# Layer 0's routing and experts in one block, weighing twenty passes behind the gate and up products

## The reference, cut to what matters

```python
scores = sigmoid(x @ gate_w.T)                       # 64 experts
grp = (scores + gate_bias).reshape(T, 8, 8)          # the best 4 of 8 groups by their two best
masked = where(group chosen, scores + gate_bias, 0)
rw = weights of the best 8 of 64, divided by their sum, x 2.5, else 0
routed = sum over e of rw[:, e] * ((silu(x @ Wg[e].T) * (x @ Wu[e].T)) @ Wd[e].T)
shared = (silu(x @ Sg.T) * (x @ Su.T)) @ Sd.T
x = layernorm(x + routed + shared)
```

## Time and profile before

| | |
|---|---|
| median of three executions | 1408.93 us |
| the profiled execution | 1402.02 us |
| its span, first to last instruction | 1400.3 us |
| busy: TensorE, VectorE, ScalarE, GpSimd | 1279.3, 1114.2, 898.5, 481.3 us |
| granted TensorE clock, mean | 0.946 |
| blocks of layer 0's routing and experts | from about 240.4 to about 692.3 us of the span |

### The profile page before, as it was taken

The page is one execution under the profiler, slowest core; times in us unless marked ns, Lnnn a source line. Parts: engine busy times, 40 slices in busy tenths (PEclk is TensorE's granted clock), DMA queues, the critical chain, the costliest instruction groups (busy, mean ns, idle before and its releaser), DMA issues. The chain is left out here.

```text
span 1400.3 us, 21389 instructions
## 1 busy us (share of the span) xinstructions
PE 1279.3 (91%) x7374; PEld 711.9 (51%) x7374; DVE 1114.2 (80%) x1726; ACT 898.5 (64%) x1503; POOL 481.3 (34%) x988
## 2 busy tenths in 40 slices
PE   5898987169999999999889999999999998999998
PEld 2222224157777777777643232223222337777776
DVE  5677763758999999999758788888889747688886
ACT  4988873034555555555453788888888866767775
POOL 4565551014334343334142244224422422221210
PEclk8898988579999999999999999999999999999999
DMA  5422200064666666666236555434342201121200
GB/s 156 127 56 66 63 21 7 0 134 110 147 143 154 148 151 151 147 146 152 79 113 146 111 156 133 121 102 104 88 123 61 53 11 52 62 91 46 91 31 31
DMA packets 70020, 135.87 MB, mean 97 GB/s; under 512 B 13031, under 2 KB 44328, under 8 KB 63112
## 3 DMA queue, kind: packets, MB, share of 16 engines
q1 hardware_dynamic: 68760, 133.46, 37.5%
q10 hardware_dynamic: 1152, 1.05, 0.2%
HBM read 116.87 MB, written 16.29 MB: 95 GB/s over the span
## 5 line engine op out<-in xcount | busy, mean ns | idle before, releaser
L1589 ACT ACTIVATE a_PR<-n1a_C 128x512 f32<-128x512 f32 x576 | 299.6, 603 | 79.5 <-PE n1a_C L1495 79.4
L1604 DVE CUSTOM_DVE_ANT_0 OC_last<-a_mring,a_COR 128x1024 bf16<-128x1024 f32 x256 | 302.6, 1218 | 42.4 <-PE a_mring L1462 42.1
L1432 POOL TENSOR_SCALAR_AFFINE_SELECT a_PR<-a_PR 128x128 f32<-128x128 f32 x512 | 136.2, 296 | 250.2 <-ACT a_PR L1589 249.7
L868 ACT ACTIVATE e_HH<-e_H 128x512 fp32r<-128x512 f32 x184 | 116.4, 633 | 158.3 <-DVE e_H L916 157.5
L1495 PE MATMUL n1a_C<-a_QP,a_KP 74*128 74x512 bf16 (+3 forms) x768 | 176.1, 332 | 4.4 <-ACT a_PR L1589 3.5
L402 ACT ACTIVATE a_PR<-a_ring,a_ng 128x1024 f32<-128x1024 f32 (+1 forms) x160 | 150.2, 1045 | 26.0 <-PE a_ring L345 26.0
L427 DVE TENSOR_SCALAR a_PR<-a_PR,a_lo,a_hi 128x1024 f32<-128x1024 f32 (+1 forms) x160 | 119.2, 763 | 56.1 <-ACT a_PR L402 55.6
L1514 PE MATMUL n1a_C<-a_PR,a_V 128*9 128x512 f32 (+3 forms) x1536 | 152.1, 492 | 0.0
L887 DVE TENSOR_TENSOR e_HL<-e_H,e_HH 128x512 fp32r<-128x512 f32 x138 | 139.4, 1010 | 13.5 <-DVE e_H L904 0.5
L810 POOL TENSOR_TENSOR e_HL<-e_H,e_HH 128x512 fp32r<-128x512 f32 x46 | 78.5, 1706 | 180.5 <-ACT e_HH L868 180.5
L1883 DVE TENSOR_TENSOR e_HL<-e_GL,e_HH 128x512 fp32r<-128x512 f32 x144 | 109.5, 765 | 38.3 <-ACT e_HH L1851 34.7
(11 more groups left out here) (257 smaller groups left out, 2252.6 us busy)
## 6 DMA issues: line engine op xcount, KB each, us to landing
e_ROUTE<-routing SPq DMA_DIRECT2D x24, 704.0 KB
a_QP<-q_parts SPq DMA_DIRECT2D x72, 192.0 KB
e_RAW<-in_w_chunks SPq DMA_DIRECT2D x46, 192.0 KB, 7.4
a_QM<-q_parts SPq DMA_DIRECT2D x64, 128.0 KB, 2.8
e_GATE<-gates SPq DMA_DIRECT2D x8, 1024.0 KB, 4.4
e_ROUTE<-routing SPq DMA_DIRECT2D x8, 640.0 KB
a_KP<-k_parts SPq DMA_DIRECT2D x24, 192.0 KB
e_ROUTE<-routing SPq DMA_DIRECT2D x8, 576.0 KB
```

What stands on the lines that cost most here:

```text
L868: nc.scalar.activation(HH[n % NH][:], HT[n % NH][:], ACT.Copy).then_inc(high_done, 1)
L1432: last = nc.gpsimd.affine_select(out=d, in_=d, compare_op=keep, fill=0.0, base=0, pattern=[[step, P]], channel_multiplier=-step)
L1589: nc.scalar.activation(PR[:, g % NPR, j, :], ring[n % NRING][:], ACT.Exp).then_inc(s_read, 1)
L1604: nc.vector.tensor_tensor_reduce(out=junk[:, i % 2, :], in0=mring[k % 2][:], in1=COR[:, c:c + S], scale=1.0, scalar=-3.0e38, op0=ALU.mult, ...
```

## The change

`moe_l0` takes the place of `route_l0` and `experts_l0`.

- **Under the normalisation** (`AheadMoeL0`): the loads of the gate weights and of chunks 0 to 3, their first splits, the logits (TensorE), the sigmoid and the high part of X (ScalarE) and its low part (GpSimd) are issued inside `normalise("n0a")`.
- **Under the routing chain**: VectorE's chain has fewer operations (maxima and minima by halves take the place of reductions and comparisons: of 15 operations on 1024 elements 9 are left, the 16 pairs stay), and after most of its steps one product (`link(..., then)`), 20 in all. TensorE runs passes 0 to 19 (gate and up) and the shared expert's down step meanwhile, which is now one float32 product from RAW and T with no split of H.
- **At pass TURN = 20** TensorE waits for the weights and turns them, into the four banks of psG and psU.
- **From then on** VectorE's turn n is: product n, the low part of n - 21, the weighing of n - 20 (in place in T; 24 T buffers instead of 2). The down step follows 23 passes behind.
- GpSimd has the low parts of all odd n, two of four groups instead of one.
- ROUTE has two buffers instead of three, RAW four, split weights eight. SyncE loads chunk c's RAW and then the ROUTE of chunk c - 9; the last nine ROUTE loads stand alone.
- In `project_l1` the wait for `cor_loaded` comes one group earlier, with 5 more `keep_busy` products there, and the 16 at the end become 5.

The remaining edits share buffers (OC, the output weights) between the layers.

```diff
+                    if ahead is not None and g >= 2:
+                        ahead.logits_of(pe, g - 2, done, base + g - 1, C[g - 2])
...
+                if ahead is not None:
+                    for g in range(NG - 2, NG):
+                        ahead.high_of_x(act, g, done, base + g + 1)
+                    for g in range(NG):
+                        ahead.scores_of(act, g, C[g])
...
+    def load_chunk(self, sp, c):
+        if c >= NRAW:
+            sp.wait_ge(self.w_split, 2 * (c - NRAW + 1))
+        if NRAW <= c < NRAW + CHS:
+            sp.wait_ge(self.down_done, (c - NRAW + 1) * NG)
+        sp.dma_start(self.RAW[c % NRAW][:], self.a["w_chunks"][c]).then_inc(self.w_loaded[c % NRAW], 16)
+    def split(self, pool, c):
+        raw, high, low = self.RAW[c % NRAW], self.WH[c % NSLOT], self.WL[c % NSLOT]
+        pool.wait_ge(self.w_loaded[c % NRAW], (c // NRAW + 1) * 16)
+        if c >= NSLOT:
+            pool.wait_ge(self.down_done, (c - NSLOT + 1) * NG)
+        self.nc.gpsimd.tensor_copy(high[:], raw[:]).then_inc(self.w_split, 1)
+        pool.wait_ge(self.w_split, 2 * c + 1)
+        self.nc.gpsimd.tensor_tensor(low[:], raw[:], high[:].bitcast(F32), ALU.subtract).then_inc(self.w_split, 1)
...
+    NR = 2
+    NH = 4
+    TURN = 20
+    BEHIND = 20
+    DOWN = BEHIND + 3
+    NTR = 24
+    NSH = CHS * NG
+    NCH = CHS + CH0
+    N = NCH * NG
+    POOL_BEHIND = 6
+    def segments(c):
+        r0 = (c - CHS) * P
+        for e in range(r0 // I0, (r0 + P - 1) // I0 + 1):
+            yield e, max(e * I0, r0) - r0, min((e + 1) * I0, r0 + P) - r0
+    def route_count(c):
+        return 16 * sum(len(list(segments(d))) for d in range(CHS, c + 1) if d % NR == c % NR)
+    def on_pool(n):
+        return n % 2 == 1
...
+                for c in range(CHS, CHS + NR):
                     load_route(c)
-                for c in range(NW, NCH):
-                    sp.wait_ge(w_split[c % NW], c // NW * 2)
-                    load(c)
-                    if c >= CHS + NW:
-                        sp.wait_ge(h_ready, (c - NW + 1) * NG)
-                        load_route(c)
+                for c in range(2 * NRAW, NCH):
+                    ahead.load_chunk(sp, c)
+                    if c - 2 * NRAW - 1 >= CHS + NR:
+                        load_route(c - 2 * NRAW - 1)
+                for c in range(NCH - 2 * NRAW - 1, NCH):
+                    load_route(c)
...
+                for c in range(ahead.FIRST, NCH + POOL_BEHIND):
+                    if c < NCH:
+                        ahead.split(pool, c)
+                    if c - POOL_BEHIND >= CHS:
+                        for n in range((c - POOL_BEHIND) * NG, (c - POOL_BEHIND + 1) * NG):
+                            if on_pool(n):
+                                low(n)
...
+                def turn_weights():
+                    pe.wait_ge(weights_ready, 1)
+                    pe.wait_ge(silu_done, TURN)
+                    pe.wait_ge(mul_done, TURN)
+                    for g in range(NG):
+                        for t in range(TG0):
+                            last = nc.tensor.transpose(banks[g][0:NE0, t * P:(t + 1) * P], rw[:, g * TG0 + t], consts["ident"][:])
+                        last.then_inc(turned, 1)
+                def down_shared(n):
+                    pe.wait_ge(mul_done, n + 1)
+                    nc.tensor.matmul(acc[n % NG][:], RAW[n // NG][:, 2, :], T[n % NTR][:], start=(n < NG), stop=True,
+                                     skip_group_check=True).then_inc(down_done, 1)
...
+                    if 3 <= n < NSH + 3:
+                        down_shared(n - 3)
+                    if n - DOWN >= NSH:
+                        down(n - DOWN)
...
+                for n in range(N + BEHIND + 1):
+                    if n == TURN:
+                        for g in range(NG):
+                            act.wait_ge(turned, g + 1)
+                            nc.scalar.activation(RT[:, grp(g)], banks[g][0:NE0, :], ACT.Copy).then_inc(kept, 1)
+                    if n < N:
+                        silu(n)
+                    if n - BEHIND - 1 >= NSH:
+                        high(n - BEHIND - 1)
...
+                def product(n):
                     dve.wait_ge(up_ready, n + 1)
                     dve.wait_ge(silu_done, n + 1)
-                    if n < NSH:
-                        h_free(n)
-                        nc.vector.tensor_tensor(HT[n % NH][:], SG[n % 2][:], psU[n % 2][:], ALU.mult).then_inc(h_ready, 1)
-                        dve.wait_ge(h_ready, n + 1)
-                        dve.sem_inc(mul_done, 1)
-                        if n:
-                            low(n - 1)
-                        continue
-                    nc.vector.tensor_tensor(T[n % 2][:], SG[n % 2][:], psU[n % 2][:], ALU.mult).then_inc(mul_done, 1)
-                    low(n - 1)
+                    if NTR <= n < NTR + NSH:
+                        dve.wait_ge(down_done, n - NTR + 1)
+                    elif n >= NTR and on_pool(n - NTR):
+                        dve.wait_ge(low_pool, low_on_pool(n - NTR))
+                    nc.vector.tensor_tensor(T[n % NTR][:], SG[n % 2][:], psU[n % 2][:], ALU.mult).then_inc(mul_done, 1)
...
+                for t in range(NT_TOK):
+                    link(v.max(top[:, t], t1[:, t]))
+                    link(v.match_replace(t2[:, t], top[:, t], t1[:, t], 1e30), t % 2)
+                link(v.scalar_tensor_tensor(t1, t2, 1e29, sc[:], ALU.is_ge, ALU.mult), 1)
+                link(v.tensor_reduce(den[:], t1, AX.X, ALU.add), 1)
+                link(v.tensor_scalar(den[:], den[:], 1e-20, 1 / ROUTED_SCALE, ALU.add, ALU.mult))
+                link(v.reciprocal(den[:], den[:]))
+                v.tensor_tensor(rw[:], t1, den[:].unsqueeze(2).to_broadcast([P, NT_TOK, NE0]), ALU.mult).then_inc(weights_ready, 1)
+                for n in range(products[0], BEHIND + NSH):
+                    product(n)
+                for n in range(BEHIND + NSH, N + BEHIND + 1):
+                    if n < N:
+                        product(n)
+                    if n - BEHIND - 1 >= NSH:
+                        low(n - BEHIND - 1)
+                    if n - BEHIND < N:
+                        weigh(n - BEHIND)
...
-                        pe.wait_ge(cor_loaded, 32)
...
+                    if g == NG - 2:
+                        pe.wait_ge(cor_loaded, 32)
+                        keep_busy(psV, 5)
...
-                keep_busy(psQ[0], 16)
+                keep_busy(psQ[0], 5)
...
-            route_l0(nc, X, a["gate_w"], a["gate_bias"], a["earlier"], consts, routing0)
-            experts_l0(nc, X, Y, routing0, a["w_chunks"])
+            ahead0 = AheadMoeL0(nc, part, X, a)
+            normalise(nc, "n0a", X, consts, signals, 0, update=output0, load_ahead=ahead0.load, ahead=ahead0)
+            moe_l0(nc, X, OC, last, ahead0, consts, routing0, part)
```

More of the change, by code:

```diff
@@ L521, in _ @@
                     nc.scalar.activation(dev_of[:, g], scale[g][:, 0:TG], ACT.Sqrt, bias=consts["eps"][:]).then_inc(dev, 1)
+                    if ahead is not None and g >= 2:
+                        ahead.high_of_x(act, g - 2, done, base + g - 1)
+                if ahead is not None:
+                    for g in range(NG - 2, NG):
+                        ahead.high_of_x(act, g, done, base + g + 1)
+                    for g in range(NG):
+                        ahead.scores_of(act, g, C[g])
+            if ahead is not None:
+                @block.gpsimd
+                def _(pool):
+                    for c in range(ahead.FIRST):
+                        ahead.split(pool, c)
+                    for g in range(NG):
+                        ahead.low_of_x(pool, g)
             @block.vector
@@ L731, in experts_l0 @@
     N = NCH * NG
-    ON_POOL = (3,)
+    POOL_BEHIND = 6
     def segments(c):
@@ new lines, in link @@
+                def link(ins, then=0):
+                    links[0] += 1
+                    ins.then_inc(step, 1)
+                    for _ in range(then):
+                        product(products[0])
+                        products[0] += 1
+                    dve.wait_ge(step, links[0])
+                by_group = ch.rearrange("p t (g e) -> p (t g) e", g=NGRP)
+                flat = lambda t: t[:].rearrange("p t g -> p (t g)")
+                wide = lambda t, k: flat(t).unsqueeze(2).to_broadcast([P, NT_TOK * NGRP, k])
@@ new lines, in _ @@
+                dve.wait_ge(ahead.loaded, 48)
+                dve.wait_ge(ahead.scored, NG)
+                link(v.tensor_tensor(ch, sc[:], ahead.bias[:].unsqueeze(1).to_broadcast([P, NT_TOK, NE0]), ALU.add))
+                v.tensor_tensor(upper, by_group[:, :, 0:4], by_group[:, :, 4:8], ALU.max)
+                link(v.tensor_tensor(lower, by_group[:, :, 0:4], by_group[:, :, 4:8], ALU.min), 1)
+                v.tensor_tensor(first, upper[:, :, 0:2], upper[:, :, 2:4], ALU.max)
+                v.tensor_tensor(other, upper[:, :, 0:2], upper[:, :, 2:4], ALU.min)
```

(7 more changed lines are left out.)

351 lines of the change are left out of this document (148 added, 203 removed).

## The result

The changed kernel takes 1440.8 us (median of three runs, 1438.3 to 1442.8) against 1408.9: ratio 1.0233, 95% interval 1.0196 to 1.0270. It is slower; whether by as much as 2%, the interval leaves open. The forecast was 1408, with a range from 1374 to 1426. Its profiled execution spans 1441.1 us, 40.8 over that of before.

A forecast was written before the change was run, and what follows sets the result against it. ROUTE loads were to pace the expert loop at 9.1 us per chunk, giving back the overlap's some 31 us; block +0.7, next normalisation +0.5 and project_l1 -2 made -1 in all: 1408 us, range 1374 to 1426.

The forecast's parts named there:

- T: Time per chunk in the expert loop when ROUTE sets the pace: taken as 9.1 us, bounds 8.5 to 9.8.
- The passes from 31 on: The prediction's part on the expert loop: ROUTE loads set the pace, 9.1 us per chunk, over TensorE's 8.2.
- a: Expert loop, from VectorE's being ready for a chunk's first weighing to the issue of the next load batch: 3.0 us.
- b: Expert loop, from a chunk's first weighing to VectorE's being ready for the next one: 6.9 us.
- L: Expert loop, from the issue of a ROUTE and RAW batch to its last landing: 8.2 us, bounds 7.2 to 9.
- the tie: SyncE's loop: a ROUTE load waits behind a RAW load, that one for GpSimd's split, that one for low parts.
- What would show it: Signs in the loop: about 2 us idle per chunk at the weighing, ROUTE batches 9.1 us apart, TensorE 90% busy.
- rival 2, Port: Expert loop: GpSimd's reads hold the port it shares with VectorE and slow VectorE, 1434 us; chance 0.13.
- A warmer clock: In project_l1: with five added fillers it cancels, leaving 2 us gained from 11 fewer fillers.
- ROUTE lands in time: Expert loop: ROUTE batches cause no wait and TensorE keeps 8.2 us per chunk, 1376 us; chance 0.23.
- The chain hides less: Routing chain: TensorE falls to half clock in the 16 pairs, a pass takes 2.7 us, 1418 us; chance 0.06.

The follow-up runs named there:

- e5: On e1, no VectorE products stand between the routing chain's steps: 1401.3 us.
- e9: On the changed kernel, the RAW loads of chunks 8 to 11 are issued ahead of the routing's stores: 1437.1 us.
- e10: On e1, the RAW loads of chunks 8 to 11 are issued ahead of the routing's stores: 1380.7 us.
- e7: On e1, project_l1's edit is undone, with 16 fillers at its end again: 1382.7 us.
- e1: On the changed kernel, SyncE's loop issues each ROUTE load ahead of the RAW load it stood behind: 1385.4 us.

## Why the prediction was wrong

**The mechanism was right.** The step that failed is the size of T in "The passes from 31 on": "two chunks take a + b + L = 18.1", and "I take 9.1". The weighing waits for ROUTE, RAW goes out right behind the split, batches wait for low parts, TensorE is 90% busy, and taking the tie away brings 8.16: all as "What would show it" has it, but two chunks take 19.7. By terms, in the 24 of chunks 5 to 36 that wait over 0.3 us (L here from ROUTE's own issue, 0.4 behind RAW's):

- a: I read it on a quiet port, 3.0 to RAW's issue, 3.4 to ROUTE's. That is what the timeline shows at 474.9 (474.22 + 0.67) to 477.90, where VectorE had stopped: its cast takes 0.50, as in rows 3. At 467.26 to 471.47 it is 4.2. The argument against rival 2, "while VectorE waits for ROUTE the port is free", fails behind a chunk that did not wait, and 8 of 32 do not. The mean is 3.83: +0.4.
- L: 7.8 by my sum, 8.68 measured: 8.2 for batches of two pieces, 9.2 for three. The mean from RAW's issue, 9.1, is over the upper bound that I gave ("at most 9"). From ROUTE's own issue it is 9.4 where the chunk ahead did not wait, and 8.3 where it did. In the first case the next batch goes out 6.4 to 7.6 us behind and the two are under way together; that this is why was not tested. +0.9.
- b: 6.9, measured 7.54 in these chunks, and 6.8 in the eight that don't wait. +0.4 on average.

Over two chunks these are 1.7 us, 0.85 each, against the 0.74 by which the period is longer; times 32 the latter is the +23.7. My own upper bound for T, 9.8, was just passed, and my range left it out: with 32 x 0.7 on top of 1408 its end stood at 1430. (The lower one is 8.35 by its own terms, 3 + 6.5 + 7.2 over two, not 8.5.)

**Ahead of the loop**, "the first ROUTE lands at about 304 ... hidden" failed. The weights were ready as forecast (42.3 us into the block against 42, which itself started 2.7 earlier than I had it, measured from the normalisation). In part that is luck: e5 shows 27.6 us for the chain alone, where I had 25.9, so that the twenty products cost 14.7 and not 16. But the first two batches go out together, and behind them RAW 8, the load of chunk 8's weights: ROUTE 2 landed at 310.3 and RAW 8 took 14 us. The tile's view of e_RAW, changed kernel, 285 to 325 us:

```profile
L668 SPq DMA_DIRECT2D e_RAW<-in_w_chunks x6: 328/434/1347, 300.6 to 322.9; - x6
...
  DMA e_RAW<-in_w_chunks: 33.5, 1
...
  PE e_psG L819: 3.1, 1
...
DMA to landing us min/median/max: 2.3/13.5/14.0
```

I had counted only ROUTE on SyncE's queue there, not the load queued behind it. The trace of before shows it already, for three RAW loads issued from 296.2 on behind three ROUTE batches. Its view of e_RAW, 294 to 325 us:

```profile
L778 SPq DMA_DIRECT2D e_RAW<-in_w_chunks x3: 327/351/422, 296.2 to 298.8; - x3
...
DMA to landing us min/median/max: 18.5/19.5/20.2
```

From the weights to chunk 4's first weighing it took 41.5 us where I had 36.6. How much of these 4.9 is RAW 8's is not shown in full: with it out of the way 0.9 us go in the tied order (e9) and 3.6 in the untied one (e10). For the rest I have no cause.

**The tail**, 6.6 us longer: "the last four chunks take 5.7 to 7.2 each" came out at 6.8 to 8.7 (the last five first weighings: 686.31, 693.38, 700.94, 707.78, 716.52). Each waits for a load that is issued after the weighing two chunks before, and the load takes 8.3 to 8.5 us to land in three of the five (chunks 41, 43 and 45), where I had 7.2.

**project_l1**, "-2": the stage is shorter, the program is not. "A warmer clock" does not show: on the untied order the granted clock at the stage's end and behind it was 0.50 with the fewer fillers and 1.00 with the old ones (e7); in the 12 us around the attention's start it was 0.71 in the changed kernel (772 to 784) and 1.00 before (738 to 750). **The rivals**: *ROUTE lands in time* gives TensorE's pace, which is what comes when the tie is undone, 1385 against its 1376; it missed the tail and RAW 8. *Port*, priced at 1434, was near the time for the wrong reason: in e1 low parts and weighings take longer still and TensorE keeps its pace; in the changed kernel they lengthen the chain that SyncE waits for. *The chain hides less* did not happen: between 260 and 275 us the granted clock was 1.00. The sentence on the Trainium skill (SBUF, State Buffer; The DMA setup-cost knee) stands: 4.9 us by the page, 7 to 10.4 measured for these batches.

## What to carry to other kernels

Look at what stands ahead of a load on its queue, not only at what the load itself waits for: here two swapped statements of SyncE's program are worth 55 us, while a third buffer in the old order is worth nothing. When a chain closes on itself through several engines, size its terms as they are while those engines are busy; and if one of them alternates between waiting and working, so do the terms. When work is moved earlier, check the loads queued behind the first one as well. And where fillers are taken out, look at the granted clock of the stage behind.
